# Queries and keys projected transposed, the rotation's sums on VectorE and the rests on GpSimd

## The reference

```
xn = layernorm(x)                               # (16, 1024, 256)
q, k, v = xn @ W_q, xn @ W_k, xn @ W_v          # 16 heads of 16
q, k = rope(q), rope(k)                         # halves of 8: q1*cos - q2*sin, q2*cos + q1*sin
s = softmax(causal(q k^T) / sqrt(16)) @ v @ W_o
h = leaky(xn @ w_fc[e], 0.5) ** 2               # e = argmax(xn @ w_router^T), one expert for each token
g = silu(h @ w_proj[e])
out = x + s * g
```

## Time and profile before

| | |
|---|---|
| median of 3 runs | 2587.51 us (2580.51 to 2588.74) |
| the profiled execution's own time | 2589.81 us |
| its span, first to last instruction | 2588.1 us |
| mean granted TensorE clock | 0.98 of full speed |

### The profile page before, as it was taken

One profiled execution on the slowest core, in us unless ns is written; L12 is line 12 of the kernel. 1 busy time (PEld: TensorE's weight loads), 2 busy tenths in 40 slices (PEclk: granted clock), 3 DMA queues, 4 the chain that ended last, 5 costly groups with the idle time before them and its releaser, 6 DMA issues. The chain is left out here.

```text
span 2588.1 us, 53564 instructions
## 1 busy us (share of the span) xinstructions
PE 2462.0 (95%) x16876; PEld 1281.0 (49%) x16877; DVE 2113.8 (82%) x6183; ACT 1746.4 (67%) x4187; POOL 988.5 (38%) x1187
## 2 busy tenths in 40 slices
PE   7999994899999999999999999999999999899886
PEld 6888872233334334334333333343333343588775
DVE  7888886899989989989989999899899899355344
ACT  5777772477777777777777777777777777555211
POOL 6888885122222222222222222222222222222666
PEclk9999996799999999999999999999999999999999
DMA  6999997654655655655556646556556552498898
GB/s 234 351 347 357 350 336 221 120 114 93 112 118 99 113 103 102 120 102 106 117 91 143 120 93 113 110 97 116 110 101 120 94 104 54 127 309 314 267 357 269
DMA packets 305865, 435.04 MB, mean 168 GB/s; under 512 B 101808, under 2 KB 204464, under 8 KB 305584
## 3 DMA queue, kind: packets, MB, share of 16 engines
q1 hardware_dynamic: 293296, 398.05, 60.7%
q0 software_dynamic: 12288, 33.57, 5.0%
HBM read 241.18 MB, written 188.74 MB: 166 GB/s over the span
## 5 line engine op out<-in xcount | busy, mean ns | idle before, releaser
L887 DVE CUSTOM_DVE_ANT_0 dump<-ps_rows,mask 128x128 bf16<-128x128 f32 (+7 forms) x2048 | 1482.0, 755 | 184.8 <-issue 151.2
L866 ACT ACTIVATE probs<-ps_cols 128x512 f32<-128x512 f32 (+3 forms) x3072 | 1275.6, 506 | 489.4 <-PE ps_cols L1035 483.5
L1035 PE MATMUL ps_cols<-q_st,k_st 99*128 99x512 bf16 (+3 forms) x3072 | 835.5, 329 | 8.2 <-DMA q_st<-max_T 3.2
L845 POOL TENSOR_SCALAR_AFFINE_SELECT probs<-probs 128x512 f32<-128x512 f32 x512 | 324.7, 634 | 1305.0 <-ACT probs L866 1304.8
L979 PE MATMUL ps_rows<-k_st,q_st 96*128 96x512 bf16 (+3 forms) x3072 | 775.5, 330 | 26.7 <-DMA v_st<-v_dram 21.2
L1011 PE MATMUL ps_ctx<-probs,v_st 128*32 128x512 f32 (+3 forms) x6144 | 615.6, 495 | 0.0
L1035 PEld LDWEIGHTS ps_cols<-q_st,k_st 99*128 99x128 bf16 x3072 | 273.7, 97 | 497.0 <-ACT probs L866 294.0
L979 PEld LDWEIGHTS ps_rows<-k_st,q_st 96*128 96x128 bf16 x3072 | 279.4, 98 | 332.7 <-DVE row_max L887 164.0
L1011 PEld LDWEIGHTS ps_ctx<-probs,v_st 128*32 128x32 f32 x6144 | 140.2, 108 | 214.6 <-ACT probs L866 77.9
L280 POOL TENSOR_TENSOR roped<-rope_c,rope_s 128x512 f32<-128x512 f32 x128 | 164.8, 1288 | 41.8 <-DVE rope_s L404 41.6
L887 DVE DVE_READ_ACCUMULATOR2_ANT row_max<- 128x1 f32 x2048 | 169.8, 83 | 0.4
(11 more groups left out here) (113 smaller groups left out, 2653.1 us busy)
## 6 DMA issues: line engine op xcount, KB each, us to landing
parts_dram<-parts SPq DMA_DIRECT2D x128, 384.0 KB, 3.8
q_st<-parts_dram SPq DMA_DIRECT2D x384, 128.0 KB, 4.2
k_st<-parts_dram SPq DMA_DIRECT2D x384, 128.0 KB, 7.0
v_dram<-v_sb SPq DMA_DIRECT2D x128, 256.0 KB, 5.4
v_st<-v_dram SPq DMA_DIRECT2D x64, 512.0 KB, 9.2
xs_dram<-zeros SPq DMA_DIRECT2D x36, 512.0 KB, 6.9
xs_sb<-xs_dram SPq DMA_DIRECT2D x72, 256.0 KB, 4.6
g_dram<-g_sb SPq DMA_DIRECT2D x72, 256.0 KB, 3.5
```

What stands on the lines that cost most here:

```text
L845: nc.gpsimd.affine_select(out=tri, in_=tri, compare_op=ALU.is_ge, fill=0.0, base=0, pattern=[[0, GH], [1, P]], channel_multiplier=-1).then ...
L866: nc.scalar.activation(probs[:, k % PB, h, 0:w], ps_cols[(GH * k + h) % CB][:, 0:w], ACT.Exp).then_inc(exp_done, 1)
L887: nc.vector.tensor_tensor_reduce(out=dump[:, even, 0:n], in0=ps_rows[:, 512 * bank:512 * bank + n], in1=mask[:, S - n:S], scale=1.0, scala ...
L1035: nc.tensor.matmul(ps_cols[(GH * k + h) % CB][:, 0:w], k_st[r][:, j // IB, h * 512 + (j % IB) * P:h * 512 + (j % IB + 1) * P], q_st[r][:, ...
```

## The change

1. **Queries and keys come out transposed.** The weights are the stationary operand and xT the moving one: `heads(m, k)` makes 128 features by 512 tokens in one PSUM bank. m = 2 t + a counts half tiles: a = 0 for queries and a = 1 for keys; k = 0 has the first halves of all heads and k = 1 the second halves. Four banks `ps_qk` serve two m. The weights' columns are put in the order half, feature, group, head while they are cut into high and low, in five pieces for each. `transpose_qk`, `ps_m` and GpSimd's sum are gone.
2. **VectorE makes four products and two sums for each m** (`rotate`), each 128x512. Two of the products go to SBUF (`rope_s`), two are written over their own operand in PSUM, and a sum reads one of either. The query's scale is an immediate in `scalar_tensor_tensor`.
3. **The rests go to GpSimd, in pieces of 1024.** `take_rest` is now GpSimd's, with `part3`; both and ScalarE's `part1` and `part2` are 128x1024, two of each for a tile. GpSimd also takes the variance and mean steps (`scale`).
4. **Smaller values.** A head has 17 columns in `v_sb`, `v_dram` and `v_st` in place of 32. The stationary slice of the product with the values still has 32 columns and so takes in some of the next head's, whose results nobody reads.
5. **SyncE's queue.** Values are stored in one DMA for a tile and parts in two of 768 KB, the parts one tile later. The 36 clears move to the attention, four in each of its first nine groups, and the scatters of xn begin at group 9.
6. **The first group's operands are loaded in the projections**, at tile 8, into buffers that live through both phases; mask and identities are made in the projections too.
7. The one-hot table is written in its own order.

```diff
+        def rotate(m):
+            t, a = divmod(m, 2)
+            u, at = m % 2, (t % TPB) * TOK
+            cos, sin = (rope_sb[:, i, at:at + TOK] for i in range(2))
+            first, second = ps_qk[2 * u], ps_qk[2 * u + 1]
+            def times(out, ps, table):
+                if a == 0:
+                    return nc.vector.scalar_tensor_tensor(out, ps[:], SCALE, table, ALU.mult, ALU.mult)
+                return nc.vector.tensor_tensor(out, ps[:], table, ALU.mult)
+            dve.wait_ge(qk_ready, 2 * m + 1)
+            times(rope_s[:, u, 1], first, sin).then_inc(product, 1)
+            times(first[:], first, cos).then_inc(product, 1)
+            dve.wait_ge(qk_ready, 2 * m + 2)
+            times(rope_s[:, u, 0], second, sin).then_inc(product, 1)
+            times(second[:], second, cos).then_inc(product, 1)
+            if m >= 2:
+                dve.wait_ge(rest_ready, m - 1)
+            dve.wait_ge(product, 4 * m + 3)
+            nc.vector.tensor_tensor(roped[:, u, 0], first[:], rope_s[:, u, 0], ALU.subtract).then_inc(qk_used, 1)
+            dve.wait_ge(product, 4 * m + 4)
+            nc.vector.tensor_tensor(roped[:, u, 1], second[:], rope_s[:, u, 1], ALU.add).then_inc(qk_used, 1)
...
     def _(pool):
+        for m in range(NM + 2):                     # NM = 2 * NT
+            if 1 <= m <= NM:
+                take_rest(m - 1)
+            if m % 2 == 0 and m // 2 + 2 < NT:
+                scale(m // 2 + 2)
+            if m >= 2:
+                part3(m - 2)
...
     def _(act):
+        for m in range(NM + 2):
+            t, a = divmod(m, 2)
+            if m < NM:
+                values(2 * m)
+                if t + 1 < NT:
+                    if a == 0:
+                        apply(t + 1, 2)
+                        apply(t + 1, 3)
+                    else:
+                        xT_hi(t + 1)
+            if m >= 2:
+                part2(m - 2)
+            if m < NM:
+                values(2 * m + 1)
+            if 1 <= m <= NM:
+                part1(m - 1)
+            if a == 1 and t + 2 < NT:
+                apply(t + 2, 0)
+                apply(t + 2, 1)
...
     def _(dve):
+        for m in range(NM):
+            t, a = divmod(m, 2)
+            if a == 0 and t + 2 < NT:
+                ln_stats(t + 2)
+                ln_aggregate(t + 2)
+            if a == 1 and t + 1 < NT:
+                xT_lo(t + 1)
+            rotate(m)
+        choose()
...
     def _(pe):
+        for m in range(NM):
+            t, a = divmod(m, 2)
+            pe.wait_ge(xT_lo_ready, DC * (t + 1))
+            values(2 * m)
+            if a == 1 and t + 1 < NT:
+                transpose_xn(t + 1, (2, 3))
+            heads(m, 0)
+            values(2 * m + 1)
+            if a == 0 and t + 1 < NT:
+                transpose_xn(t + 1, (0, 1))
+            heads(m, 1)
...
     def _(sp):
-            for i in range(CLEARS * t // NT, CLEARS * (t + 1) // NT):
-                clear_xs(i)
+            if t > 0:
+                store_parts(t - 1)
+            if t == FIRST_GROUP_AT:
+                for j in range(TPB):
+                    sp.wait_ge(v_stored[j % 2], 16 * (j // 2 + 1))
+                    sp.wait_ge(parts_stored[j % 2], 32 * (j // 2 + 1))
+                load_operands(sp, parts_dram, v_dram, 0, 0, *first_in)
             sp.wait_ge(v_ready, SUB * (t + 1))
...
-        for r in range(RING - 1):
+        for r in range(1, RING - 1):
             load(0, r)
```

More of the change, by code:

```diff
@@ L89, in project_phase @@
     slot, block_expert = tables
+    ident, ident_b, mask = consts
     NQKV = w_all.shape[1]
@@ L139, in project_phase @@
     ps_f = [bank(f"ps_f{i}") for i in range(2)]
-    ps_qk = [bank(f"ps_qk{i}") for i in range(2)]
+    ps_qk = [bank(f"ps_qk{i}") for i in range(4)]
     ps_vr = [bank(f"ps_vr{i}") for i in range(2)]
-    ps_m = [bank(f"ps_m{i}") for i in range(2)]
     x_loaded = [sem(f"x_loaded{u}") for u in range(XR)]
@@ L307, in _ @@
         act.wait_ge(w_loaded, 16)
-        nc.scalar.activation(w_all_hl[0][:], w_all_raw[:], ACT.Copy).then_inc(w_hi_cut, 1)
+        for a in range(2):
+            for c in range(DC):
+                nc.scalar.activation(cut_columns(c, a)[0], by_group(w_all_raw, a)[:, c],
+                                     ACT.Copy).then_inc(w_hi_cut, 1)
+        nc.scalar.activation(w_all_hl[0][:, :, 2 * D:], w_all_raw[:, :, 2 * D:], ACT.Copy).then_inc(w_hi_cut, 1)
         xT_hi(0)
+        apply(1, 0)
@@ new lines, in _ @@
+        dve.wait_ge(w_hi_cut, CUTS)
+        for a in range(2):
+            for c in range(DC):
+                hi, lo = cut_columns(c, a)
+                nc.vector.tensor_tensor(lo, by_group(w_all_raw, a)[:, c], hi.bitcast(F32),
+                                        ALU.subtract).then_inc(w_lo_cut, 1)
+        nc.vector.tensor_tensor(w_all_hl[1][:, :, 2 * D:], w_all_raw[:, :, 2 * D:],
+                                w_all_hl[0][:, :, 2 * D:].bitcast(F32), ALU.subtract).then_inc(w_lo_cut, 1)
@@ L733, in attention_phase, with subs_scattered @@
     block = ctx.enter_context(nc.Block())
-    LOAD = 16 * (2 * len(SLOT_Q) + 1)
-    SUBS_SCATTERED = NT * SUB // N
+    CLEARS = NBLK * BLK // (4 * P)
+    CLEAR_GROUPS = 9
+    CLEARED = CLEARS // CLEAR_GROUPS
+    def subs_scattered(n):
+        at = [NT * SUB * max(m - CLEAR_GROUPS, 0) // (N - CLEAR_GROUPS) for m in (n, n + 1)]
+        return range(*at)
     SCATTER_STEP = IB
@@ L783, in group @@
                 store_ctx(n - 1, b - (1 if r == 0 else 0), (r - 1) % RING, 1)
+            if n < CLEAR_GROUPS:
+                for i in range(CLEARED // 2):
+                    clear_xs(CLEARED * n + i)
             store_ctx(n, b, r, 0)
@@ L786, in group @@
                 load_max(n + 1, (r + 1) % RING, 0)
-            t = n // SUBS_SCATTERED + 1
-            if n % SUBS_SCATTERED == 0 and 2 <= t < NT:
-                sp.wait_ge(scattered[t % 2], 16 * SUB * (t // 2))
-                load_xn(t)
+            if n < CLEAR_GROUPS:
+                for i in range(CLEARED // 2, CLEARED):
+                    clear_xs(CLEARED * n + i)
+            for s in subs_scattered(n):
+                t = s // SUB + 2
+                if s % SUB == SUB - 1 and t < NT:
+                    sp.wait_ge(scattered[t % 2], 16 * SUB * (t // 2))
+                    load_xn(t)
             if n == EXPERT_WEIGHTS_AT:
```

444 lines of the change are left out of this document (194 added, 250 removed).

## The result

The changed kernel takes 2546.18 us (median of 4 runs, 2541.3 to 2549.72) where the kernel before took 2588.12 us beside it: a ratio of 0.9841, 95% interval 0.9826 to 0.9856, 41.9 us less. The prediction said 2532.5 us and 55.0 us less. It had the sign and the period right, and 13 us of the gain are missing. The profiled execution took 2543.15 us, with a span of 2541.4.

A forecast was written before the change was run, and what follows sets the result against it. GpSimd and ScalarE taking turns were to set the changed loop's period; before, TensorE and DMAs were full. -36.2 + 0.8 - 1.6 - 3.5 - 14.5 = -55.0 from 2589.8 gave 2534.8, as median 2532.5 us; range 2506 to 2560.

The forecast's parts named there:

- The period: Projections loop: time for each tile falls from 12.13 to 11.0 us, 36.2 us less over 32 tiles.
- The ring: Projections: GpSimd and ScalarE take turns through in-order queues, 5.0 us in a half tile without `scale` against GpSimd's own 4.4.
- Rival A: Projections: VectorE paces at 10.4 us a tile, total 2513 us, or 2507 at 10.2; chance 18%.
- Rival B: Projections: DMA landings pace at 11.5 us a tile, total 2548.5 us, or 2561 at 11.9; chance 20%.
- Rival D: Projections: VectorE stretches GpSimd's rests, at 1.5 times their cost a period of 14.4 us, total 2641 us; chance 5%.
- Rival C: Projections: something no row shows holds the period at 12.13 us, only the passage is won, total 2569 us; chance 7%.
- The loop's sum: Projections: -36.2 us from the period, +0.8 for cutting weights at the start, -1.6 at the loop's end.
- The 13 loads: First group's 1.85 MB loaded inside the projections: taken as 0 us, or +5 if the values store has no time to spare.
- The one-hot table and choosing: Between projections and attention: the table written in order costs 1.23 us instead of 4.70, -3.5 us.
- Their cover stays: Attention's start: TensorE needs GpSimd's ones, 13.86 us of work, only after 25 us of row items, so no cost.
- The passage: From projections to attention: the first group's operands are already there when the phase begins, -14.5 us.
- The clears: Attention's first nine groups: 2.1 MB more in each, taken as 0 us, at most +9.

The follow-up runs named there:

- e4_stats_dve: Changed kernel with the small variance and mean steps moved from GpSimd back to VectorE: 2622.8 us, ratio 0.9788 to the kernel before.
- e7_best: Changed kernel with first-group loads spread one to a tile, and the ones and the variance and mean steps on ScalarE: 2519.22 us, ratio 0.9735 to the kernel before.
- e10_extra_pass: Changed kernel with VectorE making one product of each tile a second time, into a spare tile: 2639.03 us, ratio 0.9803 to the kernel before.
- e5_clears_back: Changed kernel with the 36 clears issued in the projections again, none in the attention: 2545.48 us, ratio 0.9838 to the kernel before.
- e8_part1_first: Changed kernel with `part1` ahead of the second copy of values in ScalarE's queue: 2639.81 us, ratio 0.9803 to the kernel before.
- e9_best_order: `e7_best` with `part1` also ahead of the second copy of values in ScalarE's queue: 2611.93 us, ratio 0.9698 to the kernel before.
- e1_spread: Changed kernel with the first group's 13 loads issued one to a tile, tiles 8 to 20: 2622.07 us, ratio 0.978 to the kernel before.
- e6_hold_rests: Changed kernel with GpSimd's last three wide operations held until VectorE has written before_sub: 2547.48 us, ratio 0.9839 to the kernel before.
- e3_ones_act: Changed kernel with the ones in the k_st rows written by ScalarE instead of GpSimd's memsets: 2631.71 us, ratio 0.9819 to the kernel before.

## Why the prediction was right, and where it was not

**The period: right at 11.0, measured 11.02 to 11.04. That GpSimd's queue sets it is shown; that it came within 0.04 is partly luck.** Taking 0.46 us of work and the hops around it from GpSimd moved the period by 0.6 to 0.7 (`e4_stats_dve`, `e7_best`); adding 0.6 us to VectorE (`e10_extra_pass`) or 0.59 MB to the DMAs (`e5_clears_back`) moved it by nothing, and with its one wait taken away GpSimd's queue still took 10.82 (`e8_part1_first`). The two half tiles were forecast at 5.0 and 6.1 and came as 4.61 and 6.41, and those errors cancel. The ring was to add 0.6 to the odd one and adds 0.20, since instructions of ScalarE overlap more than I took (I counted from whole durations); the even one is longer since `scale` took 1.9 us with its hops, not 1.7, and 0.14 lie between the third part and the next rest. The wide operations were priced at 2.26 and 2.15 and measured 2.149 and 2.156.

**Rival A (VectorE paces): excluded here**, but close behind, 0.9 us a tile away, as `e9_best_order` and the first tiles show. **Rival B (landings pace): excluded.** With the clears back a tile had 2941 packets, 11.8 us at 64 ns each, and ran in 11.02. The rows of the kernel before had the DMAs at full share, and I let that share stand for half a bound. **Rival D (GpSimd stretched by VectorE):** right that the two get in each other's way, wrong about who and where. GpSimd's rests stayed at their price in the loop. It was VectorE's steps that were stretched, outside the loop, and beside them GpSimd's last three operations as well (2.91, and 6.16 for two). **Rival C (the loop gains nothing)** fell with the period.

**The loop's sum: -36.2 + 0.8 - 1.6 = -37.0 forecast, -33.6 measured**, with the stop inside. Without it (`e1_spread`) it would be -43.5. So the loop itself won 6.5 us more than forecast. I had multiplied one period by 32, and the ends are cheaper: in the first four tiles, while the buffers fill, VectorE paces at 10.07 to 10.09 us (some 3.8 us), and the last two have no `scale`, so that GpSimd's rests start 4.6 us apart in both halves (362.44, 367.06, 371.67, 376.30; some 3.6 us).

**The 13 loads: 0 forecast, 10 measured.** This is the largest single term that was missed. I wrote that SyncE would be held some 6 us and the DMAs 5, that the next store of values would be late by that, and that it had about a half tile to spare. SyncE's 6.8 us were right. The DMAs' 5 us were bytes at the rate of the loop; the loads ran far slower. In 120 to 130 us the share was 1.00 at 184 GB/s, and the row of the kernel before that would have told me stood in the earlier trace rows: 440 to 460 us, loads of the same kind, 1.06 at 173 GB/s, a rate at which the 1.85 MB take an estimated 10.7 us. The store behind them landed 10.9 us after its issue. I had priced "cover gone" at +5.

**The one-hot table and choosing: -3.5 forecast, +2.3 measured.** The table in its own order did save 2.9 us. But the change had put GpSimd's last rests beside VectorE's choosing, and ids_low +1.3, the two is_best +1.0 and +1.8 and before_sub +1.2 us ate it: 5.2 - 2.9 = +2.3. `e6_hold_rests` shows the cause of the last two; there the table costs 1.22, the 3.5 us of gain that were forecast. That the first two have the same cause was not tested. I had excluded this in the loop because no VectorE instruction there has two SBUF inputs, and did not ask it of the stretch behind the loop. The condition was also too narrow: `ids_low` (0.26 us before, 1.55 after), `max_parts` and, in `e4_stats_dve`, `minus_mean` read one SBUF tensor and were stretched like the others.

**The attention's start: 0 forecast, +2.1 measured.** "Their cover stays" was true of TensorE's wait for the ones, which never came, and false of VectorE's small steps beside the memset (`e3_ones_act`, -1.9). **The passage: -14.5 as forecast. The clears: 0 forecast, nothing measured that could be told from 0**, far from the +9 kept as a bound: from the first column score to the last copy of the context it took 1759.5 us before and 1760.1 after, but also 1759.9 in `e5_clears_back`, which has no clears there.

**One sign was worked out wrongly.** "The attention's first row item at 376 us" takes all 55.0 us from the phase's first DMA issue, though 14.5 of them belong to the row item; by the prediction's own sum it is 445.25 - 55.0 = 390.2. It came at 399.42, and the 9.2 us between are the loop's 3.4 and choosing's 5.8. GpSimd was busy 93% of the loop where 95% was the sign, and ScalarE did stand idle before `part2` for `take_rest`.

Open stays why the loads are slow as a burst. They write 16 partitions each, from rows of DRAM in pieces; a burst of other loads was not tried. Open too is what each transfer in flight had in the store's 10.9 us.

## What to carry to other kernels

Move work off the end of a phase by spreading it, not as a block: price a burst by its own transfers' measured rate, and count the landing of the first store queued behind it against that buffer's slack. When work is given to GpSimd, list what VectorE does beside it in the tail and in the next phase too; here operations with two SBUF inputs, and small ones that take a scalar, were made longer by up to a whole instruction of GpSimd's. And to find what paces a loop, trust a run that adds to one engine over shares: here three engines at 92 to 93% and DMAs at 89%, or 102% with the clears back, hid one bound.

## What the hardware showed that was not expected

- A DMA share of 1.02 at 344 GB/s did not slow the loop (`e5_clears_back`), while a share of 1.00 at 184 GB/s stopped it for 10 us. The same number means two things.
- A VectorE step of 4 elements took 2.14 us behind a GpSimd operation of 2.15 that started 0.04 us before it; one of 16 elements took 2.55 us beside a memset of GpSimd that reads nothing. Nothing arranges such a meeting: in `e4_stats_dve` it made one of the two small steps 0.5 to 2.2 us long in seven of 32 tiles.
- TensorE's granted clock fell to 0.58 of full speed in 130 to 140 us, a mean between its levels of 1.2 and 2.4 GHz, when TensorE was busy 1.51 of 10 us. In the next 20, at work again, it had 0.95.
